# The reciprocal of the softmax sum moved from behind its exp to the head of its value loop

## The reference

```python
q = rms_norm(hidden_states @ wq.T, q_norm_w)      # 16 heads of 128
k = rms_norm(hidden_states @ wk.T, k_norm_w)      # 4 key heads of 128
v = hidden_states @ wv.T
...                                               # rotary embedding of q and k
scores = jnp.einsum('bgrqd,bgkd->bgrqk', qg, k) * scale
scores = jnp.where(causal, scores, jnp.finfo(scores.dtype).min)
probs = jax.nn.softmax(scores.astype(jnp.float32), axis=-1).astype(q.dtype)
out = jnp.einsum('bgrqk,bgkd->bgrqd', probs, v)
return out @ wo.T

x = x + _L0_attn_ref(_layernorm(x, axis=-1), ...)
x = x + _L0_ffn_ref(_layernorm(x, axis=-1), ...)
```

## Time and profile before

| what | value |
|---|---|
| median of the six runs shown | 12011.7 us |
| lowest and highest of them | 11644.21 and 12040.93 us |
| time of the profiled execution | 11680.3 us |
| its span on the slowest core | 11678.8 us |
| PE, DVE, ACT busy, share of the span | 65%, 50%, 27% |
| granted TensorE clock, mean, of each core | 0.778 to 0.780 |
| the attention loop in the span | 1097 to 3585 us |

### The profile page before, as it was taken

The page is one execution under the profiler, slowest core; times in us unless marked ns, Lnnn a source line. Parts: engine busy times, 40 slices in busy tenths (PEclk is TensorE's granted clock), DMA queues, the critical chain, the costliest instruction groups (busy, mean ns, idle before and its releaser), DMA issues.

```text
span 11678.8 us, 104904 instructions; the slowest of 8 cores (11609.2 to 11678.8 us)
## 1 busy us (share of the span) xinstructions
PE 7601.3 (65%) x34752; PEld 3486.9 (30%) x34752; DVE 5824.0 (50%) x10080; ACT 3203.4 (27%) x3044; POOL 89.1 (1%) x102
## 2 busy tenths in 40 slices
PE   4742455444445548788888888888847667677771
PEld 2521222222222223333333333333313323233330
DVE  4156444444443455556555556555544554455531
ACT  1000111111110044444444444444432232232310
POOL 0000000000000000000000000000000000000000
PEclk9975555555557769999999989999978888788886
DMA  2200000000003312211112211112212223322225
GB/s 73 28 8 0 1 1 1 1 1 1 1 1 77 108 45 45 41 38 37 38 38 42 43 38 37 38 38 39 44 38 72 69 58 79 78 67 72 70 64 198
DMA packets 504956, 516.07 MB, mean 44 GB/s; under 512 B 10240, under 2 KB 444672, under 8 KB 494208
## 3 DMA queue, kind: packets, MB, share of 16 engines
q1 hardware_dynamic: 392032, 387.06, 10.7%
q0 software_dynamic: 112416, 122.30, 7.5%
HBM read 514.17 MB, written 117.44 MB: 54 GB/s over the span
## 4 chain that ended last, share of the span: by engine, by line
PE 24%; DVE 22%; ACT 22%; issue 18%; DMA 11%; DVEq 1%; SPq 1%; ACTq 0%; POOL 0%; POOLq 0%
PE PS L922 7%; DMA R<-uby 5%; DVE scr L702 4%; ACT scr L650 4%; PE PS L403 4%; ACT scr L655 4%; PE PS L384 4%; ACT scr L653 4%; ACT scr L651 3%; PE PS L238 3%; ACT scr L465 3%; DVE stat L454 3%; DVE R L708 3%; ACT scr L647 3%; DVE scr L815 2%
## 5 line engine op out<-in xcount | busy, mean ns | idle before, releaser
L799 PE MATMUL PS<-R 128*128 128x512 bf16 x16384 | 3609.6, 384 | 795.9 <-ACT scr L808 686.8
L922 PE MATMUL PS<-R,scr 128*128 128x512 bf16 x8192 | 1934.7, 401 | 992.9 <-DVE R L939 593.7
L799 PEld LDWEIGHTS PS<-R 128*128 128x128 bf16 x16384 | 1617.5, 99 | 2787.7 <-issue 901.5
L693 DVE SCALAR_TENSOR_TENSOR scr<-scr 128x1024 bf16<-128x1024 bf16 x768 | 940.7, 1225 | 1563.1 <-ACT scr L655 794.7
L922 PEld LDWEIGHTS PS<-R,scr 128*128 128x128 bf16 x8192 | 832.3, 102 | 2095.3 <-issue 1235.9
L647 ACT ACTIVATE scr<-scr,consN 128x1024 bf16<-128x1024 uint8 x384 | 437.9, 1140 | 3101.2 <-DVE scr L669 3101.2
L403 PE MATMUL PS<-R,scr 128*128 128x128 bf16 x2176 | 572.1, 264 | 1075.1 <-DVE scr L397 998.1
L695 DVE SCALAR_TENSOR_TENSOR scr<-scr,R 128x1024 bf16<-128x1024 bf16 x768 | 935.2, 1218 | 0.0
L465 ACT ACTIVATE scr<-PS,stat,consN 128x128 bf16<-128x128 f32 (+15 forms) x256 | 322.0, 1258 | 2122.5 <-DVE stat L459 2122.5
L702 DVE SCALAR_TENSOR_TENSOR scr<-scr 128x1024 bf16<-128x1024 uint8 x768 | 903.4, 1217 | 0.0
L646 ACT ACTIVATE scr<-scr,consN 128x1024 bf16<-128x1024 uint8 x384 | 473.3, 1233 | 1088.8 <-DVE R L708 1088.8
(11 more groups left out here) (93 smaller groups left out, 4085.0 us busy)
## 6 DMA issues: line engine op xcount, KB each, us to landing
scr<-intTh SPq DMA_DIRECT2D x128, 1024.0 KB, 6.0
intTh<-scr SPq DMA_DIRECT2D x128, 512.0 KB, 2.7
scr<-x2h SPq DMA_DIRECT2D x32, 1024.0 KB, 5.7
R<-gsc POOLq DMA_DIRECT2D x32, 1024.0 KB, 16.5
R<-usc POOLq DMA_DIRECT2D x32, 1024.0 KB, 23.6
R<-dsc POOLq DMA_DIRECT2D x16, 2048.0 KB, 15.4
scr<-x SPq DMA_DIRECT2D x16, 1024.0 KB, 4.9
scr<-x SPq DMA_DIRECT2D x32, 512.0 KB, 4.8
```

Source lines behind the costliest of these rows:

```text
L693: tvals[(uu, "A")] = em.on("vector", lambda vv, tm=tm: vv.scalar_tensor_tensor(tm[1], tm[2], 2.0, tm[1], A.mult, A.add), wait=wtb, inc=("D ...
L799: em.on("tensor", lambda t, pst=pst, tc=tc, lhs=lhs, rhs=rhs, kk=kk: t.matmul(pst[:, tc * 512:(tc + 1) * 512], lhs, rhs, start=(kk == 0), ...
L922: em.on("tensor", lambda t, tpd=tpd, i=i, h2=h2, p=p, tpp=tpp, sub=sub: t.matmul(ps_d[tpd][:, h2 * 512:(h2 + 1) * 512], ist[tpp][:, i * 25 ...
```

## The change

The reciprocal is taken out of the loop body, where it stood right behind its exp and before the value loop of the iteration before, and is emitted at the start of `emit_vloop` for the iteration whose sum it inverts. `emit_vloop` no longer gets `t_rs` as an argument; `pending` no longer holds it. `a3["rs"]` keeps the count of the last reciprocal of each of the two column pairs, and the exp that overwrites a sum column waits for it.

```diff
     a3 = {"sc": 0, "prow": [0, 0], "ppt": [0, 0], "pst": [0, 0, 0, 0],
-          "oa": 0, "ost": 0, "psot": 0}
+          "oa": 0, "ost": 0, "psot": 0, "rs": [0, 0]}
 
-    def emit_vloop(hq, qt, g, nk, t_e, t_rs, pb):
+    def emit_vloop(hq, qt, g, nk, t_e, pb):
         P_row = P_rows[pb]
+        sum_c = 14 if pb == 0 else 12
+        t_rs = em.on("vector", lambda v, sum_c=sum_c: v.reciprocal(stat[:, sum_c + 1:sum_c + 2],
+                                                                  stat[:, sum_c:sum_c + 1]),
+                     wait=[("AC", t_e)], inc=("DV", 1))
+        a3["rs"][pb] = t_rs
         tp_of = {}
...
             if a3["prow"][pb]:
                 wt_exp.append(("PE", a3["prow"][pb]))
+            if a3["rs"][pb]:
+                wt_exp.append(("DV", a3["rs"][pb]))
             sum_c = 14 if pb == 0 else 12
...
             a3["sc"] = t_e
-            t_rs = em.on("vector", lambda v, sum_c=sum_c: v.reciprocal(stat[:, sum_c + 1:sum_c + 2],
-                                                                      stat[:, sum_c:sum_c + 1]),
-                         wait=[("AC", t_e)], inc=("DV", 1))
             if pending is not None:
                 emit_vloop(*pending)
-            pending = (hq, qt, g, nk, t_e, t_rs, pb)
+            pending = (hq, qt, g, nk, t_e, pb)
             itc += 1
     emit_vloop(*pending)
```

## The result

The changed kernel took 11485.6 us in the median of 14 runs (11276.14 to 11747.78), against 11902.0 in the median of 31 runs of the kernel before. The ratio is 0.967, with a 95% interval of 0.963 to 0.971. A second comparison with the same two kernels gave 0.960 (0.954 to 0.967). So the kernel became 3 to 4% faster. Ratios are of fast executions only, while the medians hold slow ones too, in which a die is granted a lower clock in the dense stages, with any of the kernels.

A forecast was written before the change was run, and what follows sets the result against it. A ring of waits, no engine's throughput, bounds the attention loop. Reciprocal idle of 412.8 us less 2.0 for the first iteration saves 410.8: 12011.7 becomes 11600.9, say 11600 us; range 11230 to 11650.

The forecast's parts named there:

- The sum: Attention loop saving: 412.8 us of idle removed less 2.0 us that stays, 410.8 us, taken off the whole kernel time.
- what goes: VectorE's idle time ahead of the reciprocal in the attention loop, waiting for exp, disappears: 412.8 us in total.
- The first iteration: First attention iteration has no value loop to put beside exp, so its 2.0 us of idle stays.
- The cover: Attention loop: time from copies' start to next scores hides exp everywhere; tightest, a head's second iteration, leaves 0.78 us.
- rivals C and D: Attention loop, ACT and DVE on PSUM: taking turns leaves 89 us gained, chance 0.06; dearer contention gives 12245 us, chance 0.02.
- rival B: Denser attention loop raises TensorE's clock above 0.50: 136 to 365 us more saved, middle 11350 us; chance 0.06.
- The added wait: In the attention loop, exp(i) waits for the reciprocal of i-2, already covered by its wait for bias(i): cost 0.
- what is late next: After the change nothing new limits the attention loop; the remaining steps between engines keep their old lengths.
- the ring: Attention loop's cycle of waits, after the change: scores, max, mask, bias, reciprocal, copies, final scaling, transpose, scores; old lengths.

The follow-up runs named there:

- The late reciprocal: Changed kernel with the reciprocal moved from the head to the tail of the value loop, right ahead of the scaling: attention stage 2034.2 us against 2048.0.
- the grouped loop: Changed kernel with the reciprocal at the value loop's tail and four key tiles to a copy: attention stage 1446.0 us, again 1445.5; ratio to kernel before 0.915.

## Why the prediction was right, point by point

- **Where the time went.** The prediction said that exp lies alone on the path because the reciprocal stops VectorE ahead of copies that don't need it. The run with the wait put back returned the whole gain, and a second exp cost 294 us in the old order and 2 in the new one.
- **The size.** The sum had 410.8 us; measured were 440.4 in the stage. The term that was short is "what goes": I took the idle time ahead of the reciprocal and charged nothing for the instructions at its two ends. Before, bias and reciprocal stood exposed on either side of the wait: from the start of the bias to the first copy 2.65 us passed, of which 2.40 were idle, so 0.25 were instructions. Now the same two take 0.13, since they overlap. 0.12 us in 255 iterations is 31 us, and 410.8 + 31 = 441. The timelines of core 7 over all 255 iterations bear it out: without the idle time 0.25 us in the mean before, 0.13 after. That the sum then agrees within 1 us is in part chance, as small terms elsewhere offset each other: the copies are 7 us shorter in all, the scaling's wait 6 us longer. The late reciprocal, worth 14 us and not 39, shows the same overlap. The Trainium skill, "VectorE: DVE Perf Modes", section "Two Vector instructions with no wait between them", describes instructions that are held until earlier ones have finished, and others that are not; the trace agrees with the second kind here, with a start 0.06 us after that of a bias of 0.15 us.
- **The first iteration.** Its exp stays exposed, as said: PE's scores still wait once for it, 2.9 us in the changed kernel as before.
- **The cover.** The tightest iteration was said to leave 0.78 us, and the slack to grow from there. It was the right iteration, the second of a head, but read in the first head, which is not the tightest. There the changed kernel leaves 1.02 us between the end of the accumulator read (1160.58 + 0.19) and the next scores (1161.79). In the later heads it leaves 0.6, and in four of them 0.30 (1416.14 + 0.19 to 1416.63); the third iteration leaves about 0.62, hardly more. So the cover held with less to spare than was said. Exp twice fits in it all but for 2 us in the whole stage; exp four times runs out of it at short value loops, by about the computed amount.
- **Contention (rivals C and D).** Nothing lost: copies 223 ns with no exp beside them and 221 ns with one, two or four, exp 1258 ns. The Trainium skill, "PSUM — Partial Sum Buffer", section Specifications, says that ScalarE and VectorE reach PSUM in parallel at full bandwidth without a bank collision; the runs agree as far as they go: neither engine became slower, with the same 221 ns for the copies.
- **The clock (rival B).** It stayed at 0.50, the 1.2 GHz level, with PE busy 1219.33 of 2049 us, 60%.
- **The added wait and what is late next.** ACT never became late, exp starts as long after the bias as before (0.31 us in the mean), no instruction was added, and the ring is the old one without exp.
- **The time.** 11600 was forecast and 11485.6 measured. The difference comes from carrying the saving over to a median of six runs, 12011.7; with more runs the median of the kernel before was 11902.0, and 11902.0 - 411 = 11491. That this lies 5 us from the measured median is luck, since the stage saved 440 us, not 411. So is it that the lowest runs of the changed kernel, 11276 and 11277, lie 7 and 8 us from the sum made on the profiled execution, 11269.5: the lowest run of the kernel before was 11644, 36 us under that execution.

## What to carry to other kernels

On an engine that takes its instructions in order, place an instruction by when its input is ready, not by where its input is made: a reciprocal of 0.15 us that waits for another engine held up a value loop of up to 8 us that needed nothing from it. Read such a stall from the waits view, and add to it the steps of the instructions on both sides, which may overlap once the wait is gone. When a ring of engines bounds a stage, look next for fewer and longer turns of each engine: working in groups of four tiles brought 588 us here, more than the 440 from the exp taken off the path.

## What the runs showed of the hardware

- VectorE copies out of PSUM banks 4 and 5 are not slowed by ScalarE reading banks 0 to 3: 221 ns for 128x128 in the mean, with 0.3, 0.6 or 1.2 ms of exp in the loop.
- A copy of 128x512 bf16 out of PSUM takes 0.42 us, twice that of 128x128 (0.20 to 0.23), so the three tiles added cost as much as the first.
- At the 1.2 GHz level four transposes or matmuls of 128x128 in a row take 0.58 to 0.63 us of PE, while one took 264 or 274 ns in the mean in the ungrouped loop.
- In the grouped loop the granted clock was 0.52 in the mean, so it left the 1.2 GHz level only now and then:

```profile
1091.00:2536.00 1445.00, 822.21 (x5247) 523.14 (x5247) 789.43 (x2175) 346.31 (x513) 0.00 (x0) 0.52 0.00 1
```

The changed kernel's loop stayed at 0.50 throughout. What makes the difference was not tried.
